# A point-cloud layer inside a fused block: permutation matrices as the moving operand, and a drain fed from two queues

## The reference, cut to what matters

```python
inds_sorted = _sorted_indices(coords)            # 4 methods (space-filling keys), 2 batches, 1024 points
inds_list = [_window_inds(s) for s in inds_sorted]   # a window of 10 neighbours in sorted order
def _get_graph_features(feats, inds_list, perm, W_lin, b_lin):
    for inds in inds_list:                       # per method
        neigh = gather(feats, inds)              # sorted rows, windows of 10
        gf = concat([center, neigh - center])
    ...
    scores = einsum('bihd,bjhd->bhij', qh, qh) / 8     # 10 x 10 per head and point
    attn = softmax(scores); out = attn @ qh
    return out @ W_lin.T + b_lin
g1 = _get_graph_features(f0, ...)                # layer 1
h1 = lrelu(instance_norm(W_conv1 @ g1)); feats1 = h1.max(-1)
g2 = _get_graph_features(feats1, ...)            # layer 2, from layer 1's result
h2 = lrelu(instance_norm(W_conv2 @ g2)); feats2 = h2.max(-1)
```

## Time and profile before

| | us |
|---|---|
| median of 3 runs | 1067.68 (1065.52 to 1069.34) |
| the profiled execution, its whole time | 1066.81 |
| its span, first to last instruction | 1065.2 |
| layer 1: first sorting product to last statistics | 493.98 to 717.96 |
| layer 2: the same | 727.17 to 975.66 |

### The profile page before, as it was taken

How to read it: one execution, slowest core, us unless ns; L and a number is a source line. 1 busy time by engine, 2 the same in 40 slices (tenths; PEclk the granted TensorE clock), 3 DMA queues, 4 the chain that set the end, 5 groups by cost and what they waited for, 6 DMA issues and landing times. The chain is left out here.

```text
span 1065.2 us, 38584 instructions
## 1 busy us (share of the span) xinstructions
PE 1003.7 (94%) x16232; PEld 768.2 (72%) x16232; DVE 754.2 (71%) x1898; ACT 455.9 (43%) x701; POOL 438.7 (41%) x408
## 2 busy tenths in 40 slices
PE   4899789999999999999989999989889999998998
PEld 2799777796968879557876777769876666664585
DVE  7598893756648375975678999967578888996310
ACT  6243233241432314212247777752356676662010
POOL 1101263030220202200169999950378888886000
PEclk9999889999999999999999999999999999999999
DMA  8997666878778783864313222224122222221550
GB/s 333 406 387 267 223 248 255 328 285 293 298 244 346 265 325 124 311 240 114 53 27 73 69 67 67 69 62 77 30 50 60 58 57 58 57 61 30 229 246 21
DMA packets 58363, 181.40 MB, mean 170 GB/s; under 512 B 10041, under 2 KB 10793, under 8 KB 57898
## 3 DMA queue, kind: packets, MB, share of 16 engines
q1 hardware_dynamic: 55850, 171.80, 47.3%
q0 software_dynamic: 2432, 8.42, 2.2%
HBM read 150.26 MB, written 0.56 MB: 142 GB/s over the span
## 5 line engine op out<-in xcount | busy, mean ns | idle before, releaser
L535 PEld LDWEIGHTS ps<-hT,ring 128*128 128x128 f32 x2304 | 262.3, 194 | 13.3 <-ACT xc L666 6.8
L535 PE MATMUL ps<-hT,ring 128*128 128x128 f32 x2304 | 264.2, 278 | 6.6 <-ACT xc L666 6.6
L1806 POOL TENSOR_TENSOR X<-sortedT,ring 128x960 f16 (+1 forms) x84 | 156.9, 1867 | 0.0
L937 POOL TENSOR_TENSOR y_y<-y_z,sgate 128x512 f32<-128x512 f32 x16 | 20.0, 1270 | 217.0 <-DVE y_z L872 200.8
L1824 POOL TENSOR_TENSOR S<-S,den 128x480 f32<-128x480 f32 x86 | 86.6, 1007 | 37.9 <-DVE den L1743 37.9
L1831 POOL TENSOR_TENSOR PP<-S,PP 128x480 f16<-128x480 f32 x86 | 97.9, 1138 | 3.5 <-ACT PP L1615 3.5
L571 PE MATMUL ps<-wt,y_n 128*128 128x512 f32 x224 | 99.1, 595 | 0.0
L782 DVE SCALAR_TENSOR_TENSOR xc<-xpad,parg,xc 128x128 f32<-128x128 f32 x192 | 58.3, 366 | 56.4 <-ACT xc L666 55.2
L1519 PE MATMUL ps<-PT,ring 128*64 128x120 f16 x2752 | 96.1, 221 | 2.0 <-DMA PT<-P_turned 1.7
L1615 ACT CAST PP<-S 128x480 f16<-128x480 f32 x86 | 66.9, 778 | 60.9 <-POOL S L1824 54.6
L1519 PEld LDWEIGHTS ps<-PT,ring 128*64 128x64 f16 x2752 | 81.8, 110 | 14.8 <-DMA PT<-P_turned 6.1
(11 more groups left out here) (322 smaller groups left out, 1607.2 us busy)
## 6 DMA issues: line engine op xcount, KB each, us to landing
ring<-in_w_in SPq DMA_DIRECT2D x36, 2048.0 KB, 8.7
wt<-in_w_out SPq DMA_DIRECT2D x14, 2048.0 KB, 7.8
PT<-P_turned SPq DMA_DIRECT2D x344, 64.0 KB
ring<-in_w SPq DMA_DIRECT2D x8, 1024.0 KB, 12.0
ctx_chunks<-in_ctx SPq DMA_DIRECT2D x4, 1024.0 KB, 8.9
ring<-in_ctx SPq DMA_DIRECT2D x4, 1024.0 KB, 16.6
krow<-keys_scratch POOLq DMA_DIRECT2D x8, 512.0 KB, 6.4
mchunk<-in_mask_t POOLq DMA_DIRECT2D x8, 512.0 KB, 8.6
```

The costliest lines, as they stand in the source:

```text
L535: mm = nc.tensor.matmul(ps[:, bank, j * T:(j + 1) * T], weights[:, j, kc * P:(kc + 1) * P], k.hT[:, kc, :], start=kc == 0, stop=kc == KC - 1)
L1806: ins = gp.tensor_tensor(fcopy(c.X[u][:, 0, 0:1], full(cnt)), fcopy(c.fsT[:, 0, bass.ds(it * STEP, 1)], trio(start, cnt, 1)), fcopy(c.fTr[ ...
```

## The change

The sorting products are made with the one-hot matrix as the moving operand and the features as weights, so that the result has channels on partitions and needs no turning. The two batches of a tile stand next to each other and write to the two halves of the PSUM partitions. The method by method order is 0, 1, the first 256 columns of 3 (the "head"), 2, and the other 768 columns of 3 (the "rest"); layer 2 starts with the rest and the head of its first method, since those matrices are still there. ScalarE takes each phase out with four copies of 32 partitions into a new tile `gathered`, and transfers (16 rows each) carry it from there into `c.fsT`. The centre rows go to DRAM once and come back by 8 transfers, each of which reads 16 rows four times. The edges' copies go to ScalarE, spread over steps 1, 2, 3 and 5. In the drain two of the four placing transfers of a step are issued by ScalarE, TensorE applies the linear map ahead of the weighted rows from step 43 on, and the products with the centre stand ahead of the wait for ScalarE's copy. The statistics of the first 38 steps are aggregated during the drain. GpSimd makes the first differences in one piece, like the others.

```diff
-    return j // (NM * NT), j // NT % NM, j % NT
+    return j % B, j // (B * NT), j // B % NT
...
+        opening = [(0, "full")] if layer == 1 else [(0, "rest"), (0, "head")]
+        phases = opening + [(1, "full"), (3, "head"), (2, "full"), (3, "rest")]
...
         def _(sp):
             if layer == 1:
+                sp.wait_ge(n.stat, n.stats(6))
+            sp.dma_start(c.rows_kept, src[:, :]).then_inc(c.kept, 16)
+            sp.wait_ge(c.kept, 16 * layer)
+            for a in range(2):
+                for b in range(B):
+                    for r in range(2):
+                        at = b * C + (a * 2 + r) * CH
+                        sp.dma_start(c.fTr[r * C:(r + 1) * C, a * B + b, :],
+                                     bass.AP(tensor=c.rows_kept.tensor, offset=c.rows_kept.offset + at * N,
+                                             ap=[[0, NM], [N, CH], [1, N]])).then_inc(s_cc, 16)
+            if layer == 1:
                 for u in range(2):
                     sp.dma_start(c.PT[u]...).then_inc(s_zero, 16)
...
-                        for m in range(NM):
-                            at, to = b * C + (a * 2 + r) * CH, r * C + m * CH
-                            sp.dma_start(c.fTr[to:to + CH, a * B + b, :], src[at:at + CH, :]).then_inc(s_cc, 16)
...
+            for made, (i, kind, span) in enumerate(plan.evictions):
+                sp.wait_ge(s_row, row0 + made + 1)
+                ... place_sorted(sp, i, r, ...)
...
-                for q in range(4):
+                for q in range(2 if draining(it) else 4):
...
-                            mm = nc.tensor.matmul(ps[:, (i + halves[0]) % 2, pt * C:(pt + 1) * C], c.perm[:, perm_buffer(layer, j), pt * P:(pt + 1) * P],
-                                                  c.spl[:, s, t, b * C:(b + 1) * C], ...)
+                for lo, hi, bank in sorted_pieces(i, kind):
+                    for part in range(2):
+                        for x in range(B):
+                            b = sort_order(layer, j + x)[0]
+                            mm = nc.tensor.matmul(ps[b * C:(b + 1) * C, bank, 0:hi - lo], c.spl[:, part, t, b * C:(b + 1) * C], perm, ...)
...
-                weighted_rows(*lagged(PV_LAG))
-                linear(*lagged(LINEAR_LAG))
+                if isinstance(it, int) and it >= STEPS:
+                    linear(*lagged(LINEAR_LAG))
+                    weighted_rows(*lagged(PV_LAG))
+                else:
+                    weighted_rows(*lagged(PV_LAG))
+                    linear(*lagged(LINEAR_LAG))
...
+            for made, (i, kind, (begin, end)) in enumerate(plan.evictions):
+                act.wait_ge(s_ord, ord0 + plan.phase_end[i, kind])
...
+                for b in range(B):
+                    for a in range(2):
+                        rows = slice((b * 2 + a) * 2 * CH, (b * 2 + a + 1) * 2 * CH)
+                        ins = sc.mul(c.gathered[2 * i * CH:2 * (i + 1) * CH, a * B + b, begin:end], ...)
...
+            def place_half(it, ph):
+                if not inside(it) or not draining(it):
+                    return
+                act.wait_ge(s_turned, t0 + it + 1)
+                act.wait_ge(s_PV, t0 + it - 1)
+                for q in (2, 3):
+                    act.dma_start(...).then_inc(s_PT[ph % 2], 16)
...
-                if isinstance(it, int) and it == TURN_LAG:
-                    edges()
+                if isinstance(it, int) and it > STEPS:
+                    early_statistics(it)
...
-            pool.wait_ge(s_cc, cc0 + 16 * B * NHEAD * NM)
+            pool.wait_ge(s_cc, cc0 + 16 * B * NHEAD)
+            for i in range(2):
+                pool.wait_ge(c.landed[i], 32 * layer)
+            pool.wait_ge(c.head_in, 64 * layer)
```

More of the change, by code:

```diff
@@ L1236, in perm_buffer, with __init__, freed, sorted_pieces @@
     return (j if layer == 1 else PRODUCTS - 1 - j) % PERMS
+PER_METHOD = B * NT
+SPANS = {"full": (0, N), "head": (0, HEAD), "rest": (HEAD, N)}
+class SortPlan:
+    def __init__(self, layer):
+        opening = [(0, "full")] if layer == 1 else [(0, "rest"), (0, "head")]
+        phases = opening + [(1, "full"), (3, "head"), (2, "full"), (3, "rest")]
+        self.items = [(kind, i * PER_METHOD + B * t) for i, kind in phases for t in range(NT)]
+        self.consumed = {(kind, j + x): at + 1 for at, (kind, j) in enumerate(self.items) for x in range(B)}
+        here = lambda kind, j: j < PERMS and kind != "head"
+        self.builds = [(kind, j + x) for kind, j in self.items for x in range(B) if not here(kind, j + x)]
+        self.built = {build: at + 1 for at, build in enumerate(self.builds)}
+        self.evictions = [(i, kind, span) for i, kind in phases for span in ((SPANS["head"], SPANS["rest"]) if i == 2 else (SPANS[kind],))]
+        self.phase_end = {(i, kind): NT * (at + 1) for at, (i, kind) in enumerate(phases)}
+    def freed(self, kind, j):
+        if kind == "head":
+            return self.consumed.get((kind, j - (NM - 1) * PER_METHOD), 0)
+        return self.consumed["rest" if ("rest", j - PERMS) in self.consumed else "full", j - PERMS]
+PLAN = {1: SortPlan(1), 2: SortPlan(2)}
+SORT_BANKS, HEAD_BANKS = (2, 0, 2, 4), (4, None, None, 7)
+def sorted_pieces(i, kind):
+    if kind == "head":
+        return [(0, HEAD, HEAD_BANKS[i])]
+    begin = SPANS[kind][0]
+    return [(begin, begin + HALF, SORT_BANKS[i]), (begin + HALF, N, SORT_BANKS[i] + 1)]
 class CloudConstants:
@@ new lines, in _ @@
+            waited = 0
+            for at, (kind, j) in enumerate(plan.items):
+                i, t = j // PER_METHOD, sort_order(layer, j)[2]
+                if at in (0, NT // 2):
+                    pe.wait_ge(s_wc, wc0 + (1 if at == 0 else 2))
+                first, last = at % NT == 0, at % NT == NT - 1
+                if first and (i, kind) == (2, "full"):
+                    pe.wait_ge(s_row, row0 + (1 if layer == 1 else 2))
+                made = plan.built.get((kind, j + B - 1), 0)
+                if made > waited:
+                    pe.wait_ge(s_perm, perm0 + made)
+                    waited = made
+                for lo, hi, bank in sorted_pieces(i, kind):
+                    for part in range(2):
+                        for x in range(B):
+                            b = sort_order(layer, j + x)[0]
+                            perm = (c.heads[:, (j + x) % PER_METHOD, lo:hi] if kind == "head" else c.perm[:, perm_buffer(layer, j + x), lo:hi])
+                            mm = nc.tensor.matmul(ps[b * C:(b + 1) * C, bank, 0:hi - lo], c.spl[:, part, t, b * C:(b + 1) * C], perm,
+                                                  start=first and part == 0, stop=last and part == 1)
+                mm.then_inc(s_ord, 1)
@@ L1512, in weighted_rows @@
                     pe.wait_ge(s_O, t0 + it)
+                if not after(it, 1):
+                    pe.wait_ge(s_row, row0 + len(plan.evictions))
                 XR, PT = c.XR[ph], c.PT[ph % 2]
@@ new lines, in edges @@
+            def edges(it):
+                row = c.W
+                ends = lambda at, dims: fcopy(c.fsT[:, 0, at:], [[row, 4]] + dims)
+                if it == 1:
+                    for i in range(2):
+                        act.wait_ge(c.landed[i], 32 * layer)
+                    act.wait_ge(c.head_in, 64 * layer)
+                for i in {1: (0, 1), 2: (2, 3), 3: (4,)}.get(it, ()):
+                    sc.copy(c.pre[:, :, i, 0:i + LEAD + 1], c.fsT[:, :, 0:i + LEAD + 1]).then_inc(s_fs, 1)
+                    if i < LEAD - 1:
+                        sc.copy(c.pre[:, :, i, i + LEAD + 1:WIN], ends(i + LEAD, [[0, WIN - i - LEAD - 1]])).then_inc(s_fs, 1)
+                if it == 5:
+                    act.wait_ge(c.rest_in, 64 * layer)
+                    sc.copy(c.fsT[:, :, N:row], ends(N - 1, [[0, row - N]])).then_inc(s_fs, 1)
@@ L1800, in differences @@
                 last = isinstance(it, int) and it == STEPS - 1
-                if isinstance(it, int) and it == 2:
-                    pool.wait_ge(s_sc, sc0 + 8)
+                if isinstance(it, int) and it == 7:
+                    pool.wait_ge(c.rest_in, 64 * layer)
                 if last:
@@ L1836, in step @@
                 low_part(*lagged(0))
-            first_differences()
+            differences(0, 0)
             differences(1, 1)
```

153 lines of the change are left out of this document (75 added, 78 removed).

## The result

| | before | after |
|---|---|---|
| median | 1068.38 us (4 runs) | 1079.93 us (4 runs, 1077.67 to 1081.41) |
| profiled execution, span | 1066.81, 1065.2 | 1081.41, 1079.8 |

What follows compares the result with a forecast made beforehand. TensorE bounds the sortings and layer 2's loop, GpSimd layer 1's loop. Terms -1.0 - 3.6 - 4.2 - 4.3 + 0.5 = -12.6 us from 1066.8 give 1054.2, as a median 1055 us; range 1044 to 1065.

Steps and rivals of the forecast that it cites:

- Sorting products: Sorting in both layers: product pairs run side by side on the PSUM halves; 28.8 us in layer 1, 31 in layer 2.
- the fourth rival: Sorting on TensorE: pairs of 512 columns don't overlap, 54.6 us of products a layer, total 1099; chance 0.05.
- From sorted rows to the first scores: Between sorting and first scores: scores at 530.7 and 759.4; layer 1 gains 1.0 us, layer 2 3.6.
- the 21.8 us ahead: Centre rows coming back from DRAM before the first scores: four engines at 24 GB/s each, 21.8 us.
- the third rival: Centre rows before first scores: four engines at 10.5 GB/s each need 50 us, total 1109; chance 0.08.
- chain (b): Head of method 2 before layer 1's first scores: copies 1.1, transfer 2.6, differences 1.9 us; scores at 523.5.
- The first rival: Centre rows spread over all sixteen engines: layer 1's exponential 7.6 us sooner, total 1048; chance 0.25.
- step 2: Stretch from sorted rows to first scores: transfers queue on four engines; gains 1.0 us in layer 1, 3.6 in layer 2.
- Edges: First loop steps, edge copies off VectorE: step 3 to 6 in 13.5 us, not 17.7; gains 4.2 and 4.3 us.
- Drain: Loop ends: later linear maps against shorter aggregations; together 0.5 us lost, bounds 3 gained to 3 lost.
- wrong if layer 2's drain is shorter than before: A sign against the forecast, at the end of layer 2's loop, where 2.1 us lost stood against 2.05 won.

Runs made afterwards that it cites:

- e4: Changed kernel with TensorE's old order in the drain, weighted rows ahead of the linear map of the step before: 1075.15 us, ratio 1.0073.
- e6: Changed kernel with the clearing of PT and the convolution weights issued ahead of the centre rows: 1075.61 us, ratio 1.0077.
- e2: Changed kernel with the same eight centre-row transfers issued from GpSimd's queue instead of SyncE's: 1050.5 us, ratio 0.9860.
- e1: Changed kernel with the centre rows in sixteen transfers of first dimension 16 instead of eight of first dimension 4: 1055.0 us, ratio 0.9879.
- e3: Kernel before with only the edge copies moved to ScalarE, spread over steps 1, 2, 3 and 5: 1059.43 us, ratio 0.9925.
- e9: Changed kernel without the centre-row transfers and the wait for them, output not the reference's: 1050.86 us, ratio 0.9835.
- e7: Changed kernel with centre rows from GpSimd's queue and TensorE's old order in the drain: 1048.8 us, ratio 0.9825.
- e10: e7 without the early statistics, one aggregation over all steps at the end: 1053.67 us, ratio 0.9875.
- e5: Changed kernel with the eight narrow centre-row transfers issued from ScalarE's own hardware queue: 1081.04 us, ratio 1.0119.

## Why the prediction was wrong

1. **Sorting products: right.** 28.8 us were forecast in layer 1, and 29.2 came (493.81 to 523.0); 31 in layer 2, and 32.3 came. Pairs run side by side (80 of them in 16.41 us), so the fourth rival is out.
2. **From sorted rows to the first scores: this step failed, in its sum of transfers, not in its mechanism.** Four engines for the centre rows was right. The term that was mis-sized is what stands behind them, "the clearing of PT (5.6 us), and the sorted rows of methods 0 and 1 and the heads (5 us)", together with the 21.8 us ahead. The centre rows took 27, the clearing 10 and the sorted rows with the heads 11 us: 48 in place of 32. I priced each alone and at the rate of a transfer onto many partitions. But each sorted transfer goes onto 16 partitions, at 7.6 to 8.2 GB/s an engine; and on the four engines each term is stretched by what the other twelve do meanwhile. The row that could have told me was among those I used. 87 GB/s at a share of 0.52 is 10.5 GB/s an engine for transfers of 16 rows. I took it as a bound for the centre rows (the third rival, 1109), and gave the sorted rows, which have the form that row measured, the fast price. That rival's place was right and its payer wrong: the centre rows kept 21 to 26 GB/s, the sorted rows paid. Layer 2 has the same fault without the clearing: 780.10, 6.98 us worse by its stretch (4.2 in e4 and e6) where 4.3 better was forecast, and GpSimd's first differences wait for a transfer there too, where I had said they would not. The sum was also loose in small things: 517, 5.6 and 5 make 527.6 where it goes on with 528 to 529, and chain (b) adds up to 523.2, not 523.5.
3. **The first rival (spread over sixteen engines, 1048) was right about what the rest is worth.** e2 has it, 1050.5. e1 has it only in part, for the reason in step 2.
4. **Edges: right.** 13.5 us from step 3 to step 6 were forecast, 13.0 came (557.45 to 570.45 in layer 1), and 8.0 us alone in e3 against 8.5. In layer 2 of the changed kernel the same three steps gain 4.8, but only 2.13 of the loop's length is left. Steps 0 to 3 took 1.34 us longer, at a granted clock of 0.62 from 782 to 790, after TensorE had idled 11.18 us. The idling isn't the whole cause: in e2 and e9 TensorE idled 1.44 us there, the granted clock from 749 to 761 was 0.72, and these steps took 12.3 us as well (12.07 here, 10.73 before). Why the clock fell there is open. And the steps from 6 on were 4.55 instead of 4.51 us (1.31 us in all; e7 with the same loop had 4.51, so that is of the execution).
5. **Drain: the loss in layer 2 was right, the sum not.** From last scores to last map 2.52 us were lost there, forecast 2.1, with steps of 4.0 against 3.9. In layer 1 it was 0.71, forecast 1.5. The last aggregation shrank as forecast, in layer 2 from 2.50 to 0.47 us. Without the early statistics (e10) the stretch is 3.05 us longer in layer 2 and 0.65 in layer 1, where I had 2.05 and 1.1; the third us of layer 2 comes behind the aggregation, and no run explains it. The drains together gained 1.2 where I had 0.5 lost. The sentence "wrong if layer 2's drain is shorter than before" decides on what is meant: to the last map it is longer, to the end of its statistics 0.87 shorter.

With the measured sizes the account closes, though only in hindsight. Had step 2 used 48 us of queue, from 495 to 543, with scores at 545, layer 1 alone would have brought the forecast to 1069; the same stretch in layer 2, 5 us on the centre rows and 6 on what follows them, to 1080: slower. That it meets the median so exactly is luck, since layer 2's part varies by 2.7 us between executions.

## What to carry to other kernels

Price a transfer by two widths: how many engines its leading dimension gives it, and how many partitions it lands on; a rate measured at one pair isn't that of another. Then sum the time engine by engine over everything that is queued there, not transfer by transfer: what a narrow transfer costs is paid by the wide ones behind or beside it. If an issue on SyncE takes microseconds, look for slow transfers ahead of it before you move the issue to another engine. In a drain, keep a product of another step between two that are joined by a copy.

## What the runs showed that I had not expected

- The same eight narrow transfers kept 0.25 of the engines busy from SyncE's queue and all of them from GpSimd's (101.2% from 503 to 509 us), and the way there took GpSimd 6.11 us of issuing for eight.
- Busy all the time, sixteen engines moved 377 GB/s in transfers onto 128 partitions (e1), 187 in transfers onto 64, several at once (e2), and 120 to 135 in transfers onto 16 (e1).
- The time of an issue isn't its own: 32 KB took 6.72 us to issue behind the narrow transfers and the clearing, and ScalarE's eight took 12.42 us where SyncE's took 8.21, in time that ScalarE needed for its work.
- Two hardware queues share an engine packet by packet: with the centre rows on ScalarE's queue (e5) the later sorted rows on SyncE's finished before them, but nothing was won, since the four engines had the same work to do.
